# Four layers of attention and feed-forward on one Trainium2 core: layer 3's token norm, slot norm and start of the slots' loop rearranged

## The chip, the cores and the metric

The kernel runs on one NeuronCore of a Trainium2 chip. The metric is the device time of one execution in microseconds (us); lower is better. Engines are named as in the profile: PE (matrix multiply), PEld (its weight loads), DVE (VectorE), ACT (ScalarE), POOL (GpSimd), SP (SyncE, here only DMA issue).

## The reference

Four layers, each `xn = layernorm(x)` and then `x = x + attention(xn) + ffn(xn)`, on 8 batches of 512 tokens with 128 channels. The change is in the last layer and in the end of the one before:

```
xn = layernorm(x)                                  # layer 3's first norm
x  = x + L3_attn(xn) + L3_ffn(xn)

def L3_attn(x):     # channel attention, 16 heads of 8 channels
    q, k, v = split(x @ qkv_w.T + qkv_b)
    k = layernorm(k, 8 channels of a head); v = the same
    kv  = k.T @ v / 512 * temperature + attn_bias  # 8 x 8 for each head
    att = q @ kv + x
    return gelu(att @ p1_w.T + p1_b) @ p2_w.T + p2_b + x

def L3_ffn(x):      # soft mixture of 16 experts with 64 slots each
    x  = layernorm(x) * norm_g + norm_b            # a second norm of the same tokens
    se = (layernorm(slot_embeds) * slot_g + slot_b) * scale
    logits   = x @ se.T                            # 512 tokens x 1024 slots
    dispatch = softmax(logits, over tokens)
    combine  = softmax(logits, over slots)
    slots = dispatch.T @ x                         # then 16 gated experts on the slots
    return combine @ experts(slots)
```

## The kernel before

The whole state stays in SBUF: X (128 x 32 x 128), XN its norm, XT the norm transposed. Every engine has a queue of its own, written out by hand as a loop over **steps**. In a step the functions of one engine stand one behind the other, and an engine takes its instructions in order. Semaphores join the engines. Products of a softmax's stage are made as three fp32r matmuls, high with high, low with high and high with low (`m3`, L161 to L163), so each operand needs a rounded high part (written by ACT, L171) and a low part (a subtraction on DVE or POOL, L181).

**Layer 2** has `NV2 = 256` score tiles, one in a step (32 a batch). For tile v: PE scores in step v, DVE the negated row maximum (`minus_max`, L193) in v+1, ACT the exponential with its sum (L167) in v+2, DVE the reciprocal (L1631) in v+3, the normalising product in v+4 (DVE L176 or POOL L176 by turns), PE four transposes (L335) in v+5, ACT the high part (L171) in v+6, DVE the low part (L181) in v+7, PE the product with the values four steps later. Once a batch, beside these, stand layer 3's first norm of that batch (`STAT3`, `ROOT3`, `SCALE3`, `TOKENS3` steps behind `OT_AT`) and its transposes into XT.

**Layer 3's slots' loop** starts at step `S3 = NV2 + 2` and overlaps layer 2's last steps. It works on 64 tiles (8 a batch) of 128 slots by 512 tokens with the same software pipeline: `scores` at step v, `soft` v+1, `exp` v+2, `rec` v+3, `norm` v+4, `p_tr` v+5, `hi` v+6, `lo` v+7, `pv` from v+10, where step numbers are shifted by `LEAD = 33`. `scores(v)` waits until `exp(v-2)` has read its PSUM bank, since there are two banks (`S_BANK`). One of four `norm` is on POOL and three are on DVE. Into the same steps tables put each batch's **front**: the attention of layer 3 and the second norm, whose pieces are told by name and whose numbers are steps, shifted by 8 a batch:

```
F_PE = {0: "q", 1: "kv0", 2: "kv1", 14: "km", 17: "kq", 19: "p1", 21: "p2", 28: "tr"}
F_DV = {2: "kv0", 3: "kv1", 4: "s1", 8: "v1", 10: "vn", 15: "km", 18: "ta", 22: "x2", 23: "nv", 25: "xn", 30: "lo"}
F_AC = {1: "qt", 7: "sq", 9: "root", 20: "gelu", 24: "root2", 29: "hi", 30: "xnh"}
F_PO = {0: "x1", 5: "vs", 11: "gb", 26: "ngb", 31: "lo"}
```

`kv0`, `kv1` are keys and values with their bias (DVE). `s1` sums the heads of 8 channels (L189) and `vs` subtracts their mean on POOL (128 x 1024). `sq`, `v1`, `root`, `vn` scale them by the root of the variance: `root` is a Sqrt on ACT, and `newton` (L208 and the rows behind it) a reciprocal and one Newton step. `gb` applies gain and bias on POOL, `km`, `kq`, `ta`, `p1`, `gelu`, `p2`, `x2` are the attention's products and the sum into X. `nv`, `root2`, `xn`, `ngb` are the second norm of the tokens, with statistics of its own (L200, L203). `tr`, `hi`, `lo` make the operand of the scores (XTr, XL3), `xnh` and POOL's `lo` that of `pv`. `x1` adds the norm and p2's bias to X. The slots' embeddings are treated once, in `stat`, `sroot`, `snorm`, `saff`, `st`, `shi`, `slo`. The loop has `LEAD + 64 + 15 = 112` steps. Behind it come the experts' stage and the combine stage, each with a loop of its own. SP issues the layer's 14 loads (L1915) when batch 6's last scores of layer 2 are through.

## Time and profile before

| | us |
|---|---|
| median of 3 runs | 2239.09 (2236.21 to 2239.7) |
| the profiled execution | 2235.8 |
| its span, first to last instruction | 2234.0 |
| PE busy | 1940.2 (87%) |
| DVE busy | 1759.8 (79%) |
| ACT busy | 1420.7 (64%) |
| POOL busy | 1235.4 (55%) |
| mean granted TensorE clock | 0.963 |

Busy time is the time in which an engine had at least one instruction in work. A share over the whole span averages stages with different limits, so stages are read one by one: layer 2's last batch begins at about 1660 us of the span, the slots' loop's first score tile is at 1797.3, its last at 1998.3, the experts' stage starts at 2012.2 and the combine stage at about 2097.

### The profile page before, as it was taken

Reading aid. Unit: us, or ns where it says so; the run is one execution under the profiler, and the core shown is the slowest. Engines: PE = TensorE matmul, PEld = TensorE weight load, DVE = VectorE, ACT = ScalarE, POOL = GpSimd, SP = SyncE. Lnnn points to the kernel's source line nnn. Section 1 sums busy time; section 2 is a strip of 40 time slices with the busy share of each in tenths; the row PEclk is TensorE's granted clock in tenths of the full one; section 3 lists DMA queues with packets and bytes.
Section 4 is the critical chain, followed back from the end, with each engine's and each line's share of the span. In section 5 each row is a group of like instructions: output and inputs, shape, how many; then the busy total and the mean of one; then the engine's idle time right before and its main releaser. Section 6 shows DMA issues by size and latency. Waiting matters only on the chain.

```text
span 2234.0 us, 38976 instructions
## 1 busy us (share of the span) xinstructions
PE 1940.2 (87%) x13526; PEld 1475.1 (66%) x13526; DVE 1759.8 (79%) x4071; ACT 1420.7 (64%) x2801; POOL 1235.4 (55%) x1042
## 2 busy tenths in 40 slices
PE   3799899999989898588996999999999568789898
PEld 2566666666666666454683778778777346567797
DVE  8688989898888888467187888888888899873586
ACT  2578677777878777244235666667666257766575
POOL 3778777787877776157053445554445465326300
PEclk9999999999999999689997999999999789999999
DMA  3998788888888885201000000000010000002000
GB/s 105 310 312 303 260 299 284 291 280 291 279 290 284 289 300 211 86 1 37 1 6 1 1 1 1 1 1 1 1 32 1 0 0 1 1 31 69 24 1 39
DMA packets 73875, 264.14 MB, mean 118 GB/s; under 512 B 12272, under 2 KB 32240, under 8 KB 73168
## 3 DMA queue, kind: packets, MB, share of 16 engines
q1 hardware_dynamic: 72880, 255.19, 33.9%
q10 hardware_dynamic: 800, 6.46, 0.8%
q8 instruction: 109, 1.79, 0.3%
q14 instruction: 86, 0.70, 0.1%
HBM read 140.30 MB, written 121.31 MB: 117 GB/s over the span
## 4 chain that ended last, share of the span: by engine, by line
PE 39%; DVE 8%; ACT 6%; issue 2%; POOL 2%; POOLq 0%; DVEq 0%; ACTq 0%
PE PS L157 10%; PE PS L161 8%; PE PS L163 7%; PE PS L162 7%; PE PS L335 7%; ACT AR L167 2%; DVE AR L181 2%; ACT L167 1%; DVE DR L181 1%; DVE AR L185 1%; DVE PT L181 1%; ACT AR L171 1%; ACT PT L171 1%; POOL AR L176 1%; DVE AR L200 0%
## 5 line engine op out<-in xcount | busy, mean ns | idle before, releaser
L167 ACT ACTIVATE AR<-PS,AR 128x512 f32<-128x512 f32 x1008 | 687.3, 689 | 285.2 <-DVE AR L193 192.3
L193 DVE TENSOR_REDUCE AR<-PS 128x1 f32<-128x512 f32 x896 | 615.9, 688 | 119.0 <-PE PS L163 101.1
L335 PE MATMUL PS<-ident,AR 128*128 128x128 f32 x3816 | 584.4, 277 | 69.9 <-DVE PT L181 23.6
L157 PE MATMUL PS<-AR 128*9 128x512 f32 (+8 forms) x4190 | 507.7, 361 | 101.2 <-DVE AR L181 40.4
L335 PEld LDWEIGHTS PS<-ident,AR 128*128 128x128 f32 x3816 | 433.9, 142 | 182.6 <-issue 67.4
L181 POOL TENSOR_TENSOR AR<-AR 128x512 f32<-128x512 f32 (+5 forms) x326 | 396.9, 1234 | 254.8 <-DVE AR L181 96.0
L157 PEld LDWEIGHTS PS<-AR 128*9 128x9 f32 (+5 forms) x4190 | 292.3, 134 | 307.2 <-DVE AR L181 137.9
L171 ACT ACTIVATE AR<-PS 128x512 f32<-128x512 f32 (+3 forms) x612 | 357.1, 588 | 91.0 <-PE PS L335 47.6
L176 POOL TENSOR_SCALAR AR<-AR 128x512 f32<-128x512 f32 x144 | 245.3, 1704 | 290.3 <-DVE AR L1631 215.9
L171 ACT ACTIVATE PT<-PS 128x512 fp32r<-128x512 f32 x320 | 191.4, 598 | 196.2 <-PE PS L335 159.1
L181 DVE TENSOR_TENSOR PS<-PS,AR 128x192 f32<-128x192 f32 (+1 forms) x512 | 201.4, 393 | 99.3 <-PE PS L544 92.4
L181 DVE TENSOR_TENSOR AR<-PS,AR 128x512 f32<-128x512 f32 (+3 forms) x321 | 209.9, 654 | 34.8 <-PE PS L157 31.4
L181 POOL TENSOR_TENSOR AR<-XN,AR 128x192 f32<-128x192 f32 (+1 forms) x170 | 201.7, 1208 | 45.2 <-DMA XN<-scr 36.8
L181 DVE TENSOR_TENSOR PT<-PS,PT 128x512 fp32r<-128x512 f32 x320 | 217.4, 680 | 3.5 <-ACT PT L171 3.5
L544 PE MATMUL PS<-AR 128*128 128x320 bf16 (+3 forms) x1024 | 196.6, 274 | 0.0
L181 POOL TENSOR_TENSOR AR<-AR,XN 128x512 f32<-128x512 f32 x144 | 154.4, 1075 | 67.5 <-DVE AR L181 64.9
L541 PE MATMUL PS<-ident,XN 128*128 128x128 f32 x680 | 130.0, 273 | 0.0
L161 PE MATMUL PS<-MH,XNr 128*128 128x512 f32 x256 | 123.5, 482 | 5.2 <-ACT AR L167 2.8
L176 DVE TENSOR_SCALAR AR<-AR 128x512 f32<-128x512 f32 (+6 forms) x229 | 117.8, 518 | 1.3
L544 PEld LDWEIGHTS PS<-AR 128*128 128x128 bf16 x1024 | 100.8, 98 | 6.1
L161 PE MATMUL PS<-PT,VW 128*128 128x512 f32 x256 | 102.3, 399 | 1.8 <-DVE PT L181 1.8
L163 PE MATMUL PS<-MH,XNr 128*128 128x512 f32 x256 | 102.0, 398 | 0.0
(161 smaller groups left out, 2984.5 us busy)
## 6 DMA issues: line engine op xcount, KB each, us to landing
scr<-AR SPq DMA_DIRECT2D x128, 800.0 KB, 4.4
XN<-scr SPq DMA_DIRECT2D x85, 768.0 KB, 6.7
AR<-scr SPq DMA_DIRECT2D x43, 768.0 KB, 6.5
AR<-qsc SPq DMA_DIRECT2D x96, 192.0 KB
qsc<-AR SPq DMA_DIRECT2D x96, 128.0 KB, 3.3
AR<-in_wgu SPq DMA_DIRECT2D x16, 256.0 KB, 3.2
X<-in_x ACTq DMA_DIRECT2D x1, 2048.0 KB, 8.5
AR<-in_wi ACTq DMA_DIRECT2D x1, 2048.0 KB, 7.8
```

Of the source, the lines that this page charges most:

```text
L157: return pe.e.matmul(out, lhsT, rhs, start=start, stop=stop)
L161: pe.e.matmul(out, l[0], r[0], start=start, stop=False)
L162: pe.e.matmul(out, l[1], r[0], start=False, stop=False)
L163: return pe.e.matmul(out, l[0], r[1], start=False, stop=stop)
L167: return ac.e.activation(out, in_, func, bias=bias, scale=scale, accum_out=accum)
L171: return ac.e.activation(out, in_, ACT.Copy, bias=0.0, scale=1.0)
L176: return en.e.tensor_scalar(out, in0, s1, None, op0)
L181: return en.e.tensor_tensor(out, in0, in1, op)
L193: return dv.e.tensor_reduce(out, in_, AX.X, ALU.max, negate=True)
L335: return pe.e.transpose(out, in_, ident[0:k, 0:k])
L541: pe.e.matmul(out, lhsT, rhs, start=start, stop=start, is_transpose=True, skip_group_check=True)
L544: return pe.e.matmul(out, lhsT, rhs, start=False, stop=stop, skip_group_check=True)
```

## The change

- **First norm and second norm in layer 2's steps.** The second norm is no longer taken from statistics of its own. The tokens normed once have mean 0 and variance v y y (v the variance, y the root's reciprocal), so `scales` works out a second factor yy3 from them, POOL takes its root by a power, and ACT multiplies XN by it (`second`). ACT also sets X to X + norm (`sums`), which was half of `x1`. The steps of all this stand in `at3(b)`.
- **Gain and bias of the second norm** are applied on the transposed tokens (one column each), in the ACT copy `hi` and in a DVE operation `z` from PSUM; the difference `lo` goes to POOL. The slots take them in the copy out of PSUM. `nv`, `root2`, `xn`, `ngb` and one load are gone.
- **Keys and values are centred by their weights:** `wc` subtracts the head mean from the weights and the bias once, and `s1` and `vs` are gone.
- **Roots:** `root` is Ln and then Exp with scale -0.5 on ACT; `newton3` has three DVE operations where `newton` had five with a reciprocal.
- **Slots' embeddings** are treated in 30 steps ahead of S3, between layer 2's tiles (`PRE3`, and the entries with negative steps).
- **`LEAD` is 9 where it was 33**, so the loop has 88 steps. `norm` is on DVE for two tiles of four, POOL one, ACT one.
- Tiles have other places in SBUF, the banks of transposes and of `pv` are others, and a third store (XTX) holds operands of the scores.

```diff
-        STAT3, ROOT3, SCALE3, TOKENS3, TR3 = 2, 3, 5, 6, 11
+        STAT3, ROOT3, SCALE3, ROOT33, SCALE33 = 2, 3, 5, 6, 8
+        def at3(b):
+            if b < NB - 1:
+                return (6, 7, 8, 9), 11, 12, (13, 14, 15, 16), (17, 18, 19, 20)
+            return (6, 6, 6, 6), 7, 8, (9, 9, 10, 10), (11, 11, 12, 12)
-        S3 = NV2 + 2
+        S3, PRE3 = NV2 + 2, 30
...
                 dv.step(newton3(dv, y3, v3, q3))
                 dv.settle()
-                stt(dv, off3, NMV[:, 4 * b:4 * b + 4, 0], -1.0, y3, ALU.mult, ALU.mult).then_inc(n_y, 1)
+                dv.step(tt(dv, yy3, y3, y3, ALU.mult))
+                stt(dv, off3, NMV[:, 4 * b:4 * b + 4, 0], -1.0, y3, ALU.mult, ALU.mult)
+                ts(dv, up3, y3, 1.0, None, ALU.add).then_inc(n_y, 1)
+                dv.settle()
+                dv.step(tt(dv, yy3, yy3, NMV[:, 4 * b:4 * b + 4, 1], ALU.mult))
+                dv.settle()
+                ts(dv, v3, yy3, 1e-5, None, ALU.add).then_inc(n_v, 1)
+            def scales2(b):
+                newton3(dv, yy3, v3, q3).then_inc(n_y, 1)
...
+                    if r == sums[q]:
+                        act(ac, xt, xt, ACT.Identity, bias=off, scale=up3[:, q:q + 1])
+                    if r == second[q]:
+                        ins = act(ac, nt, nt, ACT.Copy, scale=yy3[:, q:q + 1])
...
-        LEAD, NV3 = 33, 8 * NB
+        LEAD, NV3 = 9, 8 * NB
...
-        F_PE = {0: "q", 1: "kv0", 2: "kv1", 14: "km", 17: "kq", 19: "p1", 21: "p2", 28: "tr"}
+        F_PE = {0: "tr", 2: "q", 3: "kv0", 4: "kv1", 13: "km", 15: "kq", 24: "p1", 26: "p2"}
+        F_DV = {2: "z", 4: "kv0", 5: "kv1", 7: "v1", 10: "vn", 14: "km", 16: "ta", 27: "x2"}
+        F_AC = {1: "hi", 3: "qt", 6: "sq", 9: "root", 10: "xnh", 25: "gelu"}
+        F_PO = {3: "lo", 5: "pb", 11: "gb", 13: "polo"}
+        I_PE = {0: "st0", 1: "st1"}
+        I_DV = {-29: "wc", -19: "sagg", -16: "snewt", 2: "slo0", 3: "slo1"}
+        I_AC = {1: "shi0", 2: "shi1"}
+        I_PO = {-26: "sgs", -18: "sroot", -10: "sm0", -8: "sa0", -6: "sm1", -4: "sa1"}
+        for i in range(8):
+            I_DV[i - 27], I_AC[i - 15] = f"ss{i}", f"sn{i}"
...
-        S_BANK, T_BANK = (5, 6), (7, 3)
+        S_BANK, T_BANK = (5, 6), (3, 4)
...
-                if 0 <= v - 4 < NV3 and (v - 4) % 4 != 1:
+                if 0 <= v - 4 < NV3 and v % 2 == 0:
                     norm(v - 4)
...
                 elif what == "root":
-                    ins = act(ac, SM[b % 2][:, 2, :], SM[b % 2][:, 1, :], ACT.Sqrt)
+                    ac.step(act(ac, tm, SM[b % 2][:, 0, :], ACT.Ln))
+                    ac.settle()
+                    ins = act(ac, tm, tm, ACT.Exp, scale=-0.5)
...
+                elif what == "z":
+                    ins = ts(dv, XL3f[:, sl], PS[:, f_bank["tr", b], :], ncol[:, 0:1], ncol[:, 1:2], ALU.mult, ALU.add)
```

How the instructions stand, at two places. PE, from layer 2's last products with the values (PT, VW) to layer 3's first score tile (operand SEH). Before:

```order
L163 MATMUL PS<-PT_01_61,VW_57 128x512
L157 MATMUL PS<-XT,AR 128x512
L335 MATMUL PS<-ident,AR 128x128 x4
L157 MATMUL PS<-AR,XT 128x256 x2
L335 MATMUL PS<-ident,AR 128x128 x4
L157 MATMUL PS<-AR,XT 128x256 x2
L157 MATMUL PS<-AR 128x128 x4
L157 MATMUL PS<-XT,AR 128x512
L157 MATMUL PS<-AR 128x512
L157 MATMUL PS<-AR,XT 128x256 x4
```

Behind the first row these are the first nine of the nineteen rows that stood between the two; now:

```order
L163 MATMUL PS<-PT_01_61,VW_57 128x512
L335 MATMUL PS<-ident,XN 128x128 x4
L161 MATMUL PS<-XTX,SEH 128x512
L162 MATMUL PS<-XTX,SEL_67 128x512
L163 MATMUL PS<-XL_71,SEH 128x512
```

One batch's four transposes are left between them. ACT in the steady loop, where a batch's `root` stands (128x128; PT is a tile's high part, `PS,AR 128x512` an exponential or, behind a table load and ahead of the root, the gelu). Before:

```order
L167 ACT_TABLE_LOAD
L167 ACTIVATE AR<-AR 128x4
L171 ACTIVATE PT_00_69<-PS 128x4x128
L167 ACT_TABLE_LOAD
L167 ACTIVATE AR<-PS,AR 128x512
L167 ACT_TABLE_LOAD
L167 ACTIVATE AR<-AR 128x128
```

Here the two roots (128x4 and 128x128) have an exponential and a high part between them, and the gelu stands some steps away with two loads of its own. Now:

```order
L171 ACTIVATE PT_00_69<-PS 128x4x128
L167 ACTIVATE AR<-PS,AR 128x512
L167 ACT_TABLE_LOAD
L167 ACTIVATE AR<-PS,AR 128x512
L167 ACT_TABLE_LOAD
L167 ACTIVATE AR<-AR 128x128
L167 ACT_TABLE_LOAD
L167 ACTIVATE AR<-AR 128x128
```

The gelu, Ln and Exp stand directly behind each other, each with a table load ahead of it, and no load stands between this Exp and the next exponential: three loads a batch where there were six.

## Rows read from the trace of the kernel before

**Rows 1.** The page, busy time, share and instructions of each engine.

```profile
PE 1940.2 (87%) x13526; PEld 1475.1 (66%) x13526; DVE 1759.8 (79%) x4071; ACT 1420.7 (64%) x2801; POOL 1235.4 (55%) x1042
```

**Rows 2.** Windows: length, busy (x count) of PE PEld DVE ACT POOL, clock, DMA.

```profile
1659.97:1724.40 64.43, 62.42 (x346) 51.10 (x345) 54.73 (x132) 44.43 (x105) 32.25 (x21) 1.00 0.07 21
1724.40:1797.30 72.90, 41.32 (x149) 28.59 (x148) 61.58 (x133) 21.04 (x33) 37.60 (x23) 0.74 0.00 0
1797.30:1998.60 201.30, 159.75 (x765) 119.27 (x764) 178.18 (x430) 144.97 (x271) 95.15 (x59) 0.94 0.03 9
1998.60:2012.20 13.60, 11.19 (x56) 8.23 (x54) 6.67 (x15) 6.50 (x14) 1.72 (x1) 1.00 0.00 0
```

**Rows 3.** Tiles VW and SEH: min/median/max ns, first and last start in us.

```profile
L163 PE MATMUL PS<-PT,VW x256: 387/392/628, 1233.6 to 1748.4; 128*128 128x512 f32 x128
L161 PEld LDWEIGHTS PS<-XTr,SEH x64: 186/190/337, 1797.3 to 1998.3; 128*128 128x128 f32 x64
```

**Rows 4.** Windows of one steady period of the slots' loop (8 steps).

```profile
1877.17:1905.37 28.20, 23.00 (x114) 16.90 (x114) 27.05 (x65) 22.08 (x40) 14.39 (x9) 1.00 0.00 1
```

**Rows 5.** Timeline of PE (start, duration in us), within one step.

```profile
1867.48 0.60 PE L335 MATMUL PS<-ident,AR 128*128 128x128 f32 x4
1867.83 0.48 PE L161 MATMUL PS<-XTr,SEH 128*128 128x512 f32 x1
...
1868.62 0.60 PE L335 MATMUL PS<-ident,XN 128*128 128x128 f32 x4
```

**Rows 6.** Timeline of ACT beside one token operation of layer 2's steps.

```profile
1703.12 0.49 ACT L167 ACTIVATE XN<-X,AR 128x128 f32<-128x128 f32 x1
...
1703.80 0.60 ACT L171 ACTIVATE PT<-PS 128x512 fp32r<-128x512 f32 x1 [0.19 <-PE PS L335]
```

**Rows 7.** Timeline of DVE and PE, layer 3's statistics between layer 2's tiles.

```profile
1695.43 0.87 DVE L200 BATCH_NORM_STATS2 AR<-X 128x6 f32<-128x128 f32 x4
...
1697.66 0.63 PE L335 MATMUL PS<-ident,AR 128*128 128x128 f32 x4 [0.90 <-DVE PT L181]
...
1699.70 0.47 DVE L176 TENSOR_SCALAR AR<-AR 128x512 f32<-128x512 f32 x1
```

**Rows 8.** Timeline of SP and DVE around the layer's loads.

```profile
1663.13 0.43 SPq L1915 DMA_DIRECT2D AR<-in_slots  x1
...
1666.87 0.69 DVE L176 TENSOR_SCALAR AR<-PS 128x512 f32<-128x512 f32 x1 [0.41 <-PE PS L157]
```

**Rows 9.** DMA issues, 1600 to 1760: size, median us from issue to landing.

```profile
AR<-in_slots SPq DMA_DIRECT2D x1, 512.0 KB, 4.5
```

**Rows 10.** Groups on DVE by form, 1848.84 to 1877.17: count | busy us, mean ns | idle.

```profile
L176 DVE TENSOR_SCALAR AR<-AR 128x512 f32<-128x512 f32 x6 | 4.4, 728 | 0.0
L189 DVE TENSOR_REDUCE AR<-AR 128x128 f32<-128x1024 f32 x2 | 2.4, 1209 | 0.0
L177 DVE TENSOR_SCALAR XN<-XN,AR 128x128 f32<-128x128 f32 x4 | 1.1, 341 | 0.0
L208 DVE RECIPROCAL AR<-AR 128x128 f32<-128x128 f32 x1 | 0.9, 936 | 0.0
L200 DVE BATCH_NORM_STATS2 AR<-XN 128x6 f32<-128x128 f32 x4 | 0.9, 276 | 0.0
L181 DVE TENSOR_TENSOR AR<-AR 128x4 f32<-128x4 f32 x3 | 0.8, 257 | 0.1
```

**Rows 11.** Groups on ACT and POOL by form, the same stretch.

```profile
L167 ACT ACT_TABLE_LOAD x6 | 7.7, 1283 | 0.1
L171 ACT ACTIVATE XNH<-XN 128x512 fp32r<-128x512 f32 x1 | 0.6, 645 | 0.0
L181 POOL TENSOR_TENSOR AR<-AR 128x1024 f32<-128x1024 f32 x3 | 6.8, 2262 | 4.4 <-DVE AR L181 2.6 <-DVE AR L176 1.8
L181 POOL TENSOR_TENSOR X<-X,XN 128x512 f32<-128x512 f32 x1 | 1.3, 1271 | 0.0
```

**Rows 12.** Waits, 1848.84 to 1905.37: us in total, times, longest us.

```profile
PE PS L161 <- ACT AR L167: 6.6, 8, 1.2
```

More of the change, by code:

```diff
@@ L1425, in program @@
         nst2 = A2.take(4, 6)
-        v3, q3, y3, off3, half3 = (A2.take(4) for _ in range(5))
+        assert A2.top <= 39440
+        A2.top = 39440
+        v3, q3, y3, off3, up3, yy3 = (A2.take(4) for _ in range(6))
+        half = A2.take(8)
+        nst, nmv, ny, nv_, ntm, soff = A2.take(8, 6), A2.take(8, 2), A2.take(8), A2.take(8), A2.take(8), A2.take(8)
+        cm = A2.take(64)
         XTb = XT[:, :].rearrange("p (b t) -> p b t", b=NB)
@@ L1756, in l2_po @@
             po.wait_ge(ld[2], 48)
-            po.step(po.e.memset(half3, -0.5))
+            po.step(po.e.memset(half, -0.5))
             po.settle()
@@ L1894, in program @@
+        in_turn = lambda at: [use for u in range(-PRE3, STEPS3) for use in at[u]]
+        cnt_pe, cnt_dv, cnt_ac, cnt_po = ({use: i + 1 for i, use in enumerate(in_turn(t))} for t in (at_pe, at_dv, at_ac, at_po))
+        taken_by = in_turn(at_pe)
         f_bank = {use: i % 3 for i, use in enumerate(taken_by)}
@@ L1927, in front @@
                     pe.wait_ge(ld[3], NL3)
-                if what == "q":
+                if what == "tr":
+                    pe.wait_ge(n_xd, V3 + 2 * b + 2)
+                    for q in range(4):
+                        ins = tr(pe, ps[:, q * 128:q * 128 + 128], XN[:, 4 * b + q, :])
+                elif what == "q":
                     pe.wait_ge(n_xt, XT3 + b + 1)
@@ L2083, in front @@
+                elif what[:2] == "ss":
+                    i = int(what[2])
+                    ins = dv.e.bn_stats(nst[:, i, :], SE[:, i, :])
+                elif what == "sagg":
+                    dv.wait_ge(f_dv, cnt_dv["ss7", 0])
+                    for i in range(8):
+                        dv.step(dv.e.bn_aggr(nmv[:, i, :], nst[:, i, :]))
                     dv.settle()
                     ins = ts(dv, nv_, nmv[:, :, 1], 1e-5, None, ALU.add)
-                elif what == "snorm":
-                    dv.wait_ge(f_ac, cnt_ac["sroot", 0])
-                    dv.wait_ge(f_dv, cnt_dv["stat", 0])
-                    dv.step(newton(dv, ny, nv_, ntm))
+                elif what == "snewt":
+                    dv.wait_ge(f_dv, cnt_dv["sagg", 0])
+                    dv.wait_ge(f_po, cnt_po["sroot", 0])
+                    dv.step(newton3(dv, ny, nv_, ntm))
@@ L2089, in front @@
                     dv.settle()
[L2090 to L2098 removed]
+                    ins = stt(dv, soff, nmv[:, :, 0], -1.0, ny, ALU.mult, ALU.mult)
@@ L2206, in step @@
                     exp(v - 2)
+                if 0 <= v - 4 < NV3 and v % 4 == 3:
+                    m = (v - 4) % 8
+                    ac.wait_ge(s3_rc, v - 3)
+                    act(ac, PB3[(v - 4) % 4], PB3[(v - 4) % 4], ACT.Copy, scale=DN3[:, m:m + 1]).then_inc(nd3_ac, 1)
                 for what, b in at_ac[u]:
```

326 lines of the change are left out of this document (173 added, 153 removed).

## Prediction

> **What bounds the kernel now.** The busy shares of the whole span [rows 1] name PE first, but they average stages with different limits. So the windows by stage come next [rows 2]. In layer 2's last batch PE is busy 62.4 of 64.4 us: PE bounds that stage, one step takes 2.01 us, and DVE has 9.7 us free there, ACT 20. In the 72.9 us behind it PE is busy 41.3 us, at a granted clock of 0.74 of 2.4 GHz, ACT 21.0 and DVE 61.6. That is a gap: layer 2's last product starts at 1748.4 and layer 3's first score tile at 1797.3 [rows 3], and between them stands little but the fronts of the first batches, a chain in which DVE is taken most. In the 201.3 us of score tiles DVE is busy 178.2. The reading is sharper in one period of 8 steps, which is one batch [rows 4]: 28.20 us, DVE busy 27.05, PE 23.0, ACT 22.1, POOL 14.4. DVE bounds the loop. PE's 23.0 holds its short waits in part, since a matmul's end is modelled: from start to start, four transposes take 0.35 us and a product of three matmuls 0.79 us [rows 5]. By that a step's own products are 0.35 + 2 x 0.79 = 1.93 us, or 15.4 a period, and the front adds about 6, which makes 21, against the 23.0 of the window; I take 22 as PE's work in a period.
>
> **The sum, stage by stage**, against the profiled execution's own 2235.8 us.
>
> *Layer 2's steps.* ACT gets eight token operations more a batch (`sums`, `second`). A token operation takes 0.49 us, and behind one of today's ACT still sat idle 0.19 us for PE [rows 6], so one in a step costs nothing, and `at3` puts them one to a step; if that cover were gone, it would be up to 0.3 us each. DVE gets 8 small operations more a batch, at about 0.2 us each with their waits. Today's statistics of a batch, 1.45 us more in one step, made PE wait 0.90 us [rows 7]; the new ones are 1.0 us in one step and 0.6 three steps on, and I take 0.3 us a batch, 2.4 in all. POOL's second power falls into the half of its steps where it has no product. The slots' work ahead of S3 adds: `wc` some 1.5 us of DVE in one step, `sagg` 1.2, `snewt` in the same step as batch 6's statistics, and four steps in which ACT has two extra operations. Each is paid in part: 2 us. `wc` and POOL's `sgs` wait for all loads, and behind `wc` stand layer 2's next row maxima, so a late load would stop PE. The last load issues at 1663.13 today and one load fewer makes it about 0.5 us earlier [rows 8]; it lands 4.5 us later [rows 9], at 1667.2. `wc` stands one step behind the operation at 1666.87 [rows 8], so at about 1669: hidden, with 1.5 us to spare. Sum: **+4 us**, between 0 (all hidden, as ACT's is) and +12 (every DVE addition paid in full).
>
> *The gap.* What stands ahead of the first score tile now is layer 2's last ten products (10 x 0.7), its last transposes, one batch's front up to `kv1`, the slots' transposes and the second batch's `tr`: 12 us of PE work from 1724.4 by the spacings of [rows 5]. The chain beside it (transposes, `hi`, `z`, POOL's `lo`) is short, since statistics, roots and slots are done. With hand-overs I take 18.6 us, so the first tile at **1743**, not 1797.3. Ends: 1736 (PE's work alone) and 1750 (right behind where the last product stands today [rows 3]).
>
> *The loop's first 15 steps* (tiles 0 to 14, fronts filling up, layer 2's last batch of statistics and tokens between them): DVE has 33 us there by the groups' durations. I take **37 us**, between 30 (layer 2's step) and 53 (today's period).
>
> *Six steady periods*, to tile 63. On DVE go from each period [rows 10]: the second norm's statistics and products (0.9 + 1.1 + 0.8, and 1.0 of small ones), one of two sums over heads (1.2 + 0.2), the reciprocal of 128 x 128 and a product behind it (1.1 net), two of six normalising products (1.46). `lo` goes and `z` comes, from PSUM and of the same size. That is 27.2 - 7.8 = 19.4 us. On ACT three table loads go (3.85), a small root goes; two copies of 128 x 512 for a product each come (1.3, by XNH's row) and Ln for 0.3: 22.1 to 19.9 [rows 4, 11]. On POOL one of three 128 x 1024 goes (2.26), `x1`'s half (1.27), and `ngb`, two of that size (2.6), and `lo`, one of it, comes [rows 11]: 14.4 a period [rows 4] becomes about 12 at most. On PE nothing goes. So PE, with 22 us, is the longest, and DVE and ACT stand at 19 to 20 close below. What is late next is the exponential. In one step of eight ACT has gelu, Ln and Exp behind one another with three loads, some 5.8 us with `hi` (3 x 1.283, two operations of the size of XNH's and two of 0.3), where today two loads at most stood between two tiles' work. `scores(v)` waits for `exp(v-2)`, and DVE's `vn` waits for the root. Followed step by step from the end of PE's `p1`, PE would reach its fourth step at 8.6 us and the exponential that it needs comes at 11.1; two steps on it has caught up to a loss of about 2 us. POOL then has `gb`, `lo`, `pb` and `polo` (8.4 us) ahead of a normalising product, which costs PE about half a microsecond more. So **24.5 us** a period, **147** for six, between 21.9 (DVE with its wait for the root) and 28.2 (nothing gained).
>
> *The tail.* From the last score tile to the experts' stage 13.6 us [rows 2]; now `p1`, gelu and `p2` of two batches stand in it: **15 us**.
>
> The experts' stage would start at 1743 + 37 + 147 + 15 = 1942, plus 4, so 1946, where it starts at 2012.2. That is 66 us less. The stages behind it keep their instructions. The profiled time becomes 2235.8 - 66 = 2169.8. The runs shown have a median 3.3 us above the profiled execution, so I predict **2173 us**.
>
> **Two rules of the Trainium skill.** The rows give 1283 ns for a table load [rows 11], and the order of instructions has one ahead of the Ln and one ahead of the Exp, three a batch. The Trainium skill, "ScalarE: Activation LUTs", section on table sets, says that Ln and Exp share one set and need one load between them. By that rule each period would have one load less; six of them make 7.7 us, and the sum would be 2165. The instructions decide, so the term stands.
>
> A normalising product on DVE takes 728 ns on the mean in the loop [rows 10] and 0.47 us where POOL is not at work beside it [rows 7]. This is what the third rival rests on. The Trainium skill, "SBUF — State Buffer", holds that DVE and GpSimd share a port pair that is locked for a whole instruction, so that the loser blocks fully; by that rule the trace agrees.
>
> **The rivals.**
> - *The loop stays at today's period.* The exponential's chain (two banks, three engines in turn) bounds it and not any engine's work. For: ACT's block is the longest single hold-up so far, and PE waits for ACT's exponentials already, 6.6 us in two periods [rows 12]. Against: those waits were behind a DVE that was 96% busy. Then 1743 + 42 + 6 x 28.2 + 15 + 4 = 1973, 39 us less: **2200 us**.
> - *PE alone sets the pace,* ACT's block is caught up in full, and the fp32 work runs at a granted clock of 1.0 throughout. For: layer 2 runs at 97% PE. Then 1743 + 32 + 6 x 22 + 14 + 3 = 1924, 88 us less: **2151 us**.
> - *The port.* Each of the four normalising products left on DVE falls beside a POOL instruction of 2.26 us and waits 1.1 us for it: DVE has 19.4 + 4.4 = 23.8 us and with its wait for the root 26.5 a period. Then 1954 + 4: 54 us less, **2185 us**.
> - *Slower.* ACT's block and POOL's eight microseconds line up, so that each batch's front comes late for the one behind it and the score tiles wait once a batch for all of it. The point at which nothing is gained: 1743 + 37 + 6P + 15 + 4 = 2012.2, so P = 35.5 us. That is 13.5 us of waiting over PE's 22. The block is 5.8 us and POOL's row 8.4, which must be paid in full, one behind the other. At P = 37 the time is 2239 + 9 = **2248 us**.
>
> **How the numbers follow.** Chances: forecast 0.55 (periods of 23.5 to 26, 2167 to 2182), today's period 0.15, PE's pace 0.15, the port 0.10, slower 0.05. The range goes from 2149 (the second rival) to 2204 (the first, with the upper end of layer 2's cost); it leaves out the slower case and what lies beyond both ends. A measurement of this kernel tells 0.2%, 4.5 us, from no change. Of the slower case 0.01 lies within that. Faster by over it is 0.95, the same 0.01, slower 0.04.
>
> **What the changed kernel's profile would show.** Right: the first score tile between 1736 and 1750; a period of about 24.5 us with PE busiest and DVE under 85%; three table loads a period; the granted clock at 1.0 between layer 2 and the loop; the experts' stage beginning near 1946; layer 2's last batch at 64 to 67 us. Wrong: a wait of DVE for a load near 1668, PE idle for ACT's exponential by more than 3 us a period, or DVE's 128 x 512 products near 1.5 us each.

## The result, and the profile after

| | before | changed |
|---|---|---|
| median (lowest to highest) | 2238.16 us (2236.21 to 2239.7, 4 runs) | 2209.34 us (2207.55 to 2211.95, 4 runs) |
| ratio, 95% interval | | 0.9873 (0.9855 to 0.989) |
| span of the profiled execution | 2234.0 | 2206.1 |
| mean granted TensorE clock | 0.963 | 0.961 |

The change gains 28.8 us, 1.3%. Forecast were 66 us: the sign was right, the size was not, and the time lies 5 us outside the range. The page's first line of the changed kernel, beside [rows 1], shows where work went: 64 us less on DVE, 18 more on ACT, 21 less on POOL.

```profile
PE 1930.2 (87%) x13526; PEld 1470.1 (67%) x13526; DVE 1695.3 (77%) x3928; ACT 1438.9 (65%) x2874; POOL 1214.8 (55%) x1033
```

The same tiles as in [rows 3], of the changed kernel (duration min/median/max in ns, first and last start in us): the last product of layer 2, the score tiles of batches 0 to 2 and of 3 to 7, and the experts' first copies.

```profile
L163 PE MATMUL PS<-PT,VW x256: 387/392/402, 1235.7 to 1745.2; 128*128 128x512 f32 x128
L161 PEld LDWEIGHTS PS<-XTX,SEH x24: 186/190/337, 1745.8 to 1822.7; 128*128 128x128 f32 x24
L161 PEld LDWEIGHTS PS<-XTr,SEH x40: 186/190/289, 1825.8 to 1963.0; 128*128 128x128 f32 x40
L171 ACT ACTIVATE HV<-AR x32: 612/620/635, 1984.0 to 2053.2; 128x512 fp32r<-128x512 f32 x32
```

From these starts the difference comes apart:

| stage | before | changed | difference |
|---|---|---|---|
| to the first score tile | 1797.3 | 1745.8 | -51.5 |
| first to last score tile | 201.0 | 217.2 | +16.2 |
| last score tile to the experts' first copy | 13.9 | 21.0 | +7.1 |
| from there to the end | 221.8 | 222.1 | +0.3 |
| sum | | | -27.9 |

So the gap ahead of the tiles closed as forecast, and 23 of its 51 us were given back behind it. The stretches of the changed kernel, in windows (length; busy us and count of PE, PEld, DVE, ACT, POOL; clock; DMA share; GB/s): the first 15 tiles, the six periods to the last tile, and the tail. DVE, busy 27 of 28 us in [rows 4], is no longer the bound of the periods: 118.33 of 170.40 us. In the first 15 tiles it is still the busiest engine, with 38.21 of 46.80.

```profile
1745.80:1792.60 46.80, 36.11 (x159) 26.20 (x158) 38.21 (x91) 34.88 (x72) 24.27 (x15) 0.85 0.00 1
1792.60:1963.00 170.40, 138.46 (x672) 107.46 (x671) 118.33 (x242) 119.01 (x225) 69.08 (x40) 0.93 0.00 1
1963.00:1984.00 21.00, 14.77 (x79) 11.16 (x77) 7.40 (x15) 12.80 (x20) 1.72 (x1) 1.00 0.17 52
```

The six periods take 28.4 us each, as long as the 28.2 of [rows 4], with another engine in front. One of them, windowed between two score tiles that follow the block of table loads:

```profile
1853.09:1880.46 27.37, 21.93 (x115) 17.08 (x114) 20.08 (x42) 20.22 (x38) 11.96 (x7) 1.00 0.00 1
```

PE's work is the 22 us that the prediction took, and DVE and ACT stand at 20 as forecast. What is left is idle time of PE: over the six periods it is idle for 31.9 us, all of it in waits for ACT's exponential. The timeline of PE has it, three waits a period for ACT's exponential, in square brackets at the row's end:

```profile
1860.18 0.50 PE L161 MATMUL PS<-XTr,SEH 128*128 128x512 f32 x1 [3.49 <-ACT AR L167]
...
1865.00 0.50 PE L161 MATMUL PS<-XTr,SEH 128*128 128x512 f32 x1 [0.98 <-ACT AR L167]
...
1876.21 0.50 PE L161 MATMUL PS<-XTr,SEH 128*128 128x512 f32 x1 [0.98 <-ACT AR L167]
```

3.49 + 0.98 + 0.98 = 5.45 us, and 21.93 + 5.45 is the window. ACT in the same step:

```profile
1853.09 1.28 ACT L167 ACT_TABLE_LOAD   x1
1854.38 0.69 ACT L167 ACTIVATE AR<-PS,AR 128x512 f32<-128x512 f32 x1
1855.09 1.28 ACT L167 ACT_TABLE_LOAD   x1
1856.38 0.31 ACT L167 ACTIVATE AR<-AR 128x128 f32<-128x128 f32 x1
1856.71 1.28 ACT L167 ACT_TABLE_LOAD   x1
1858.00 0.31 ACT L167 ACTIVATE AR<-AR 128x128 f32<-128x128 f32 x1
1858.22 0.76 ACT L167 ACTIVATE XTr<-PS,AR 128x512 fp32r<-128x512 f32 x1
1858.88 0.58 ACT L171 ACTIVATE PT<-PS 128x512 fp32r<-128x512 f32 x1
1859.36 0.69 ACT L167 ACTIVATE AR<-PS,AR 128x512 f32<-128x512 f32 x1
```

These are gelu, Ln and Exp with a load ahead of each, `hi` of the tokens, `hi` of the transposes, and then the exponential of 1859.36, on which PE's tile at 1860.18 waits: 6.3 us from the first load to it.

There is one more loss. Windows of the step behind that wait, in four periods one after the other:

```profile
1831.41:1837.64 6.23, 5.25 (x21) 4.07 (x21) 4.47 (x8) 1.78 (x5) 5.70 (x3) 0.76 0.00 0
1860.18:1865.00 4.82, 3.84 (x20) 2.82 (x20) 4.37 (x8) 1.79 (x5) 4.29 (x2) 1.00 0.00 0
1887.56:1894.02 6.46, 5.48 (x20) 3.69 (x21) 4.38 (x8) 1.79 (x5) 5.93 (x3) 0.74 0.00 1
1916.58:1922.89 6.31, 5.33 (x20) 4.15 (x21) 4.46 (x8) 1.78 (x5) 5.79 (x3) 0.75 0.00 0
```

The same work takes 4.82 us at a granted clock of 1.00, and 6.2 to 6.5 where the mean granted clock of the step is 0.74 to 0.76, that is, part of it at 1.2 instead of 2.4 GHz. Three of these four steps pay 1.4 to 1.6 us. The same step one period before them (1801.3 to 1808.9) took 7.60 us at 0.62. Work, waits and clock make the 28.4 us of a mean period: 21.9 + 5.45 + about 1. That mean holds a lighter last period of 26.3 us; the other five take 28.8, of which the clock is then about 1.5.

### The profile page after: what moved, and what is told of

Its sections match the earlier page's. It is cut to its first block, busy times and chain, and to the rows that moved or that the text cites. A ratio compares the mean times of both kernels' runs of the same rounds, so it can differ in the third digit from the quotient of the medians.

```text
span 2206.1 us, 38904 instructions
## 1 busy us (share of the span) xinstructions
PE 1930.2 (87%) x13526; PEld 1470.1 (67%) x13526; DVE 1695.3 (77%) x3928; ACT 1438.9 (65%) x2874; POOL 1214.8 (55%) x1033
## 4 chain that ended last, share of the span: by engine, by line
PE 41%; ACT 6%; DVE 5%; issue 2%; POOL 1%; DMA 0%; POOLq 0%; DVEq 0%; ACTq 0%; SPq 0%
PE PS L157 11%; PE PS L161 8%; PE PS L335 7%; PE PS L163 7%; PE PS L162 7%; ACT AR L167 3%; ACT L167 1%; ACT PT L171 1%; DVE DR L181 1%; DVE AR L185 1%; DVE PT L181 1%; POOL AR L176 1%; ACT AR L171 1%; POOL X L181 0%; DVE AR L200 0%
## 5 line engine op out<-in xcount | busy, mean ns | idle before, releaser
L167 ACT ACTIVATE AR<-PS,AR 128x512 f32<-128x512 f32 x1024 | 698.1, 689 | 288.1 <-DVE AR L193 191.6
L157 PE MATMUL PS<-AR 128*9 128x512 f32 (+8 forms) x4190 | 502.0, 360 | 86.6 <-DVE AR L181 38.0
L181 POOL TENSOR_TENSOR AR<-AR 128x512 f32<-128x512 f32 (+6 forms) x331 | 396.6, 1214 | 257.5 <-DVE AR L181 103.1
L171 ACT ACTIVATE AR<-PS 128x512 f32<-128x512 f32 (+3 forms) x596 | 347.4, 587 | 85.2 <-PE PS L335 46.9
L176 POOL TENSOR_SCALAR AR<-AR 128x512 f32<-128x512 f32 (+1 forms) x146 | 246.4, 1688 | 281.9 <-DVE AR L1643 199.4
L181 DVE TENSOR_TENSOR PS<-PS,AR 128x192 f32<-128x192 f32 (+1 forms) x512 | 201.4, 393 | 99.9 <-PE PS L544 93.0
L181 DVE TENSOR_TENSOR AR<-PS,AR 128x512 f32<-128x512 f32 (+3 forms) x321 | 210.2, 655 | 37.4 <-PE PS L157 33.7
L181 POOL TENSOR_TENSOR AR<-XN,AR 128x192 f32<-128x192 f32 (+1 forms) x170 | 201.5, 1206 | 50.5 <-DMA XN<-scr 41.2
L181 DVE TENSOR_TENSOR PT<-PS,PT 128x512 fp32r<-128x512 f32 x320 | 217.8, 681 | 13.2 <-ACT PT L171 13.0
L181 POOL TENSOR_TENSOR AR<-AR,XN 128x512 f32<-128x512 f32 x144 | 154.3, 1074 | 66.3 <-DVE AR L181 63.4
L162 PE MATMUL PS<-MH,XL 128*128 128x512 f32 x256 | 101.1, 395 | 0.0
```

Of the source, the lines that this page charges most:

```text
L157: return pe.e.matmul(out, lhsT, rhs, start=start, stop=stop)
L162: pe.e.matmul(out, l[1], r[0], start=False, stop=False)
L167: return ac.e.activation(out, in_, func, bias=bias, scale=scale, accum_out=accum)
L171: return ac.e.activation(out, in_, ACT.Copy, bias=0.0, scale=1.0)
L176: return en.e.tensor_scalar(out, in0, s1, None, op0)
L181: return en.e.tensor_tensor(out, in0, in1, op)
```

## The experiments

The theory after the result: **PE is the longest engine of the loop, so it can't make up any wait, and the time that it waits behind ACT's block of three table loads, with the slow clock around it, is lost once a batch.** Rivals: the ring of scores, maximum, exponential and transposes sets the period whatever PE does; the shorter lead of the scores (`LEAD` 9 for 33) gains nothing itself; the clock is a matter of its own. All times below come with their own runs of the kernel before; ratios are against it, and the changed kernel stands at 0.9873.

**1. No table loads.**

```diff
-                    ac.step(act(ac, tm, SM[b % 2][:, 0, :], ACT.Ln))
+                    ac.step(act(ac, tm, SM[b % 2][:, 0, :], ACT.Tanh))
-                    ins = act(ac, HG, PS[:, f_bank["p1", b], :], ACT.Gelu, bias=cols3[:, 1:2])
+                    ins = act(ac, HG, PS[:, f_bank["p1", b], :], ACT.Tanh, bias=cols3[:, 1:2])
```

> The changed kernel with Tanh in the place of Gelu and of Ln in layer 3's front: the three table loads of a period are gone, every other instruction keeps its place and size (the output is not the reference's). Theory (ACT's block of gelu, Ln and Exp with three loads holds up the exponentials, and PE cannot catch up what it idles): the wait of 3.5 us falls to under 0.5, the period from 27.4 to 23.5 to 24 us, the time by 26 to 30 us to about 2181. Rival 1 (the chain scores, maximum, exponential through two banks sets the pace whatever ACT does between): the period stays within 0.5 us of 27.4 and the time within 5 us of 2209. Rival 2 (PE catches up in the steps behind a hold-up, so its length hardly counts): a gain of under 10 us.

Measured 2172.68 us (2168.45 to 2173.56), ratio 0.9708 (0.9694 to 0.9722): 36.7 us faster than the changed kernel. More than the 26 to 30 us expected. Tanh stands where Gelu and Ln stood, so this kernel leaves out the gelu and the right roots and serves for its time alone. First to last score tile 180.6 us (217.2); the first 15 tiles, which the expectation left out, give 5.8 of it (41.0 for 46.8). A period, in a window, and the wait in the gelu's step:

```profile
1841.83:1865.30 23.47, 21.90 (x114) 17.00 (x114) 19.73 (x41) 16.08 (x35) 11.82 (x8) 1.00 0.00 1
1889.17 0.50 PE L161 MATMUL PS<-XTr,SEH 128*128 128x512 f32 x1 [0.73 <-ACT AR L167]
```

PE's busy time is the same 21.90; its wait in the gelu's step is 0.73 us, one of 0.98 is left, and the clock is at 1.00. 37 us is more than the loads' own 31 us (8 x 3 x 1.28), and about as much as the whole error of the forecast. That the period can fall to 23.5 us rules out a ring that sets 28.4 whatever ACT does between.

**2. The root by a power on POOL** instead of ACT's Ln and Exp, 128x128 in one instruction, with its wait for `v1`.

```diff
-                elif what == "root":
-                    ...
-                    ac.step(act(ac, tm, SM[b % 2][:, 0, :], ACT.Ln))
-                    ac.settle()
-                    ins = act(ac, tm, tm, ACT.Exp, scale=-0.5)
+                elif what == "root":
+                    ...
+                    ins = tt(po, SM[b % 2][:, 1, :], SM[b % 2][:, 0, :], bc(half[:, 0:1], [128, 128]), ALU.pow)
```

> The changed kernel with the root taken by a power on POOL (128x128) where Ln and Exp stood on ACT; two loads a period are left, both of the gelu. Theory: the block falls by 1.9 us (one load, Ln and Exp), PE's longest wait from 3.5 to about 1.6 us, the period to 25.5, the time by about 15 us to 2194, if the power takes under 3 us of POOL. Rival 1 (two banks): no change within 5 us. Against both: a power on 128x128 that takes POOL over 5 us a batch would hold gb and km up and make the kernel slower.

Measured 2299.62 us (2294.51 to 2300.72), ratio 1.0275 (1.0259 to 1.029): slower by far. POOL's timeline:

```profile
1860.96 20.75 POOL L181 TENSOR_TENSOR AR<-AR 128x128 f32<-128x128 f32 x1 [4.97 <-DVE AR L177]
```

One power takes 20.75 us, 0.16 us a column, and the periods become 38 to 40 us. The kernel is slower, as the expectation had it for a power of over 5 us. Its time says nothing of the theory, since POOL now holds everything up; it shows that POOL is no place for this root. PE's wait behind the gelu's two loads that are left is 1.66 to 1.68 us, near the 1.6 expected.

**3. The gelu four steps from the root.**

```diff
-        F_PE = {0: "tr", 2: "q", 3: "kv0", 4: "kv1", 13: "km", 15: "kq", 24: "p1", 26: "p2"}
+        F_PE = {0: "tr", 3: "kv0", 4: "kv1", 6: "q", 13: "km", 15: "kq", 28: "p1", 30: "p2"}
-        ... 27: "x2"}
-        F_AC = {1: "hi", 3: "qt", 6: "sq", 9: "root", 10: "xnh", 25: "gelu"}
+        ... 31: "x2"}
+        F_AC = {1: "hi", 6: "sq", 7: "qt", 9: "root", 10: "xnh", 29: "gelu"}
```

> The changed kernel with p1, gelu, p2 and x2 four steps later (and q two to four steps later, so that its buffer is free): the block becomes two, root with two loads and gelu with two loads, four loads a period. Theory (a hold-up costs PE what it exceeds some 2.3 us by): waits of 1.6 and 0.9 us where 3.5 stood, the period 1 us shorter, the tail 3 us longer, so the time 3 to 7 us shorter, about 2204. Rival (what counts is ACT's total, now one load more): 1.3 us more a period, the time 10 us longer.

Measured 2199.92 us (2198.21 to 2203.1), ratio 0.9835 (0.982 to 0.985): 9.4 us faster, more than the 3 to 7 expected, with four loads a period in place of three. PE's waits are 2.3, 0.6 and 0.98 us a period, 3.9 in all for 5.45. The waits expected of the two blocks were 1.6 and 0.9 us; the first is longer. So the number of loads is not what counts here, but how much of them stands in one block ahead of an exponential.

**4. The root by Sqrt and a longer Newton step on DVE.** Ln, settle and Exp become one Sqrt, `newton3` becomes `newton` (5 operations in place of 3).

```diff
-                    ac.step(act(ac, tm, SM[b % 2][:, 0, :], ACT.Ln))
-                    ac.settle()
-                    ins = act(ac, tm, tm, ACT.Exp, scale=-0.5)
+                    ins = act(ac, tm, SM[b % 2][:, 0, :], ACT.Sqrt)
...
-                    dv.step(newton3(dv, y1, v1, tm))
+                    dv.step(newton(dv, y1, v1, tm))
```

> The changed kernel with that one part undone: Sqrt on ACT and the reciprocal with five operations on DVE in the place of Ln, Exp and three operations. Theory: loads and block nearly the same (0.3 us less on ACT, 1.2 us more on DVE, before z): within 5 us of 2209. Rival (DVE's work still sets the pace): 1.2 us a period, 10 us longer, 2219.

Measured 2206.7 us (2204.15 to 2209.11), ratio 0.9863 (0.9847 to 0.988): 2.6 us less, which these runs don't tell from nothing. The load back to the exponential's table now stands behind both `hi`, and it is a load all the same; PE's longest wait is 3.3 us for 3.5. DVE has room for the longer step.

**5. The scores 33 steps behind the first front step again** (`LEAD, NV3 = 33, 8 * NB`), all else as changed.

> The changed kernel, with the scores 33 steps behind the slot layer's first step again, as before the change, instead of 9; everything else of the change stays. Theory (the gain of the change lies in the shorter lead, and part of it is given back because the last 24 steps now have the token work beside them): first slot tile at 1785 to 1797 us (1745.8 in the changed kernel); from first to last tile 200 to 206 us (217.2), since three periods lose their token work; the experts' first copy 14 us behind the last tile (21.0), since the token work is long over when the last tile comes; in all 15 to 27 us slower than the changed kernel, 2224 to 2236 us. Rival (the gain lies in the instructions taken out of the slot layer, not in the lead): from first to last tile 190 us or less, and within 8 us of the changed kernel, 2203 to 2217 us.

Measured 2230.51 us (2226.56 to 2233.12), ratio 0.9969 (0.9956 to 0.9982): 21 us slower than the changed kernel, so three quarters of the change's net gain are its shorter lead. The first tile comes at 1800.5 us, no earlier than before the change, although DVE has less to do there. Fronts alone are a chain of hand-overs: in 55 us PE is busy 33, at a clock of 0.66, and nobody is full.

```profile
1745.00:1800.00 55.00, 33.20 (x94) 19.96 (x93) 30.45 (x60) 26.70 (x41) 27.24 (x17) 0.66 0.00 1
```

The loop is 191.6 us there, shorter than the 200 to 206 expected and near the rival's 190; the whole time, 2230.51 us, lies in the theory's range and outside the rival's. So the instructions taken out do shorten the loop, by 9.4 us against the 201.0 of the kernel before, as long as the lead is the old one. The tail is 14.5 us as expected. What the shorter lead costs the loop is thus 26 us, what it costs the tail 6.5, and what it brings ahead of the first tile 55.

**6. One load less** (gelu as Tanh alone, as in 1; Ln and Exp stay).

> The changed kernel with Tanh in place of Gelu in the slot layer, so one of the three table loads of ScalarE's block is gone, and the two around the logarithm stay (the output differs). Theory (TensorE idles at the block's exponential, and the clock that falls behind that idle time is part of the price): the wait of TensorE for the exponential at that step falls from 3.5 us to 1.3 to 1.9 us, the granted clock stays at 1.00 behind it in all six periods, the period goes from 28.4 to 25 to 26.5 us, in all 13 to 22 us faster than the changed kernel: 2187 to 2196 us. Rival 1 (each load costs the same share of what the kernel without loads gained, 36.7 us over three loads): 12 us faster, 2197 us, with the clock still falling in some periods. Rival 2 (only the first load of the block, or the last, matters since TensorE waits for ScalarE wherever one is): within 4 us, 2205 to 2213 us.

Measured 2198.51 us (2193.15 to 2199.52), ratio 0.9822 (0.9801 to 0.9843): 10.8 us faster. As in experiment 1, Tanh leaves out the gelu. This is the first rival, an equal share for each load with the clock still falling in some periods, and not my 13 to 22 us. PE's timeline behind the block:

```profile
1829.00 0.50 PE L161 MATMUL PS<-XTr,SEH 128*128 128x512 f32 x1 [2.47 <-ACT AR L167]
...
1855.36 0.68 PE L161 MATMUL PS<-XTr,SEH 128*128 128x512 f32 x1 [2.46 <-ACT AR L167]
```

The wait fell by 1.0 us only, and the clock still fell in every second of these steps (windows 0.75, 1.00, 0.74, 1.00). From start to start of this tile the periods are 27.8, 26.4, 28.0, 26.4 and 27.3 us: 26.4 where the clock holds and 1.5 more where it doesn't. In the changed kernel the same five starts lie 30.1, 28.8, 27.4, 29.0 and 28.2 us apart. A load of 1.28 us taken away is thus 1.0 us of wait, and the mean of the five periods falls by 1.5 us (27.2 for 28.7), so that about half a microsecond of it is the clock, which falls in fewer of them.

**7. The experts' first weights earlier.** Their room is free once the last keys, values and skip sums are out, and not only behind `p2`:

```diff
-            sp.wait_ge(f_pe, cnt_pe["p2", NB - 1])
-            sp.wait_ge(f_dv, cnt_dv["km", NB - 1])
-            sp.wait_ge(f_po, cnt_po["gb", NB - 1])
+            sp.wait_ge(f_pe, max(cnt_pe["q", NB - 1], cnt_pe["kv1", NB - 1]))
+            sp.wait_ge(f_dv, cnt_dv["kv1", NB - 1])
+            sp.wait_ge(f_po, cnt_po["pb", NB - 1])
...
+                if e == 0:
+                    sp.wait_ge(f_po, cnt_po["gb", NB - 1])
+                    sp.wait_ge(f_dv, cnt_dv["km", NB - 1])
+                    sp.wait_ge(f_pe, cnt_pe["p2", NB - 1])
```

> The changed kernel, with the first expert's weights asked for as soon as the last key and value products and the last skip sum are done (their room is free then), instead of behind the last product of the token work. Theory (the 7 us that the stretch from the last slot tile to the experts' first copy has grown by are in part ScalarE's wait of 3.07 us for that transfer): the wait is gone, the experts' first copy comes 3 us earlier, in all 2 to 4 us faster, 2205 to 2207 us. Rival (the copy waits for something else next, the last slots' product or VectorE's last parts): within 1 us of the changed kernel, 2208 to 2210 us.

Measured 2204.23 us (2203.62 to 2206.22), ratio 0.9855 (0.9834 to 0.9877): 5.1 us less by the medians. The tail, from the last score tile to the experts' first copy, is 17.9 us for 21.0: 3.1 us, as much as the wait was and inside the 2 to 4 expected. The rest of the 5.1 lies ahead of the last tile, where the edit changes nothing (1961.5 for 1963.0). In ACT's timeline of the changed kernel the copy waits for the transfer; with the early request it waits no more, and the second copy 0.63 us.

```profile
1983.96 2.26 ACT L171 ACTIVATE HV<-AR 128x512 fp32r<-128x512 f32 x4 [3.07 <-DMA AR<-in_wgu]
```

```profile
1979.45 1.15 ACT L171 ACTIVATE HV<-AR 128x512 fp32r<-128x512 f32 x2
1981.22 1.15 ACT L171 ACTIVATE HV<-AR 128x512 fp32r<-128x512 f32 x2 [0.63 <-DMA AR<-in_wgu]
```

**8. Edits 3 and 7 together.**

> The kernel with the gelu four steps from the root (run before: 2199.9 us), and the first expert's weights asked for early as well. The two edits touch different stretches, so their gains should add: 2196 to 2198 us, faster than both kernels of the change. Rival (the last stretch of that kernel, 23.1 us, is set by the token work that now ends later, so the early transfer gives nothing): 2199 to 2201 us.

Measured 2198.11 us (2193.75 to 2201.37), ratio 0.9824 (0.9801 to 0.9846): 1.8 us less than with edit 3 alone (0.9835). The intervals overlap, so the times alone leave open whether the early request gains there. In the two traces the tail is 19.4 us (1956.1 to 1975.6) for 23.1 (1951.6 to 1974.7), which speaks against the rival: the transfer's wait of 5.82 us ahead of the first copy is gone, and one of 2.17 us for DVE's sums into X is left.

**9. The deciding one: another order on PE in one step of eight.** In the step that waits 3.5 us, `p2`, `q` and the values' product stood behind the waiting scores in PE's queue, and none of them needs the exponential.

```diff
+                late = u % 8 == 2
-                if 0 <= v < NV3:
+                if 0 <= v < NV3 and not late:
                     scores(v)
                 for what, b in at_pe[u]:
                     front(what, b)
                 g, j = divmod(v - 10, 4)
                 if 0 <= g < 2 * NB:
                     pv(g, j)
+                if 0 <= v < NV3 and late:
+                    scores(v)
```

> The changed kernel with TensorE's order changed in one step of eight, the one whose scores wait 3.5 us for the exponential behind ScalarE's three table loads: there the token work's products (second product of the gelu, queries) and the step's share of the values' product are issued ahead of the scores instead of behind them. Nothing is added or taken out. Theory (what TensorE loses in a period is that wait, since it has no slack to make it good, and the half clock behind it): these products are about 3.1 us of work that needs no exponential, so the wait falls from 3.5 us to 0.3 to 0.8 us, the granted clock stays at 1.00, and the period goes from 28.4 to 24.5 to 25.5 us; over some seven periods 20 to 27 us faster than the changed kernel, 2182 to 2190 us. Rival (the ring of scores, maximum, exponential and transposes sets the period, TensorE's idle time only shows where it is late): the scores of that step come later by what was put ahead of them, the wait moves on to the next steps, and the time is within 6 us of the changed kernel, 2203 to 2215 us.

Measured 2187.25 us (2186.86 to 2191.78), ratio 0.9776 (0.9752 to 0.9799): 22 us faster than the changed kernel, inside the 20 to 27 expected, from instructions that are the same in number and kind. PE's timeline, to be held against the rows around 1860.18 above:

```profile
1851.91 0.60 PE L335 MATMUL PS<-ident,AR 128*128 128x128 f32 x4
1852.35 1.06 PE L157 MATMUL PS<-AR 128*128 128x128 f32 x8
1853.24 1.02 PE L157 MATMUL PS<-XT,AR 128*128 128x512 f32 x2
1853.70 0.79 PE L161 MATMUL PS<-PT,XNH 128*128 128x512 f32 x1
...
1855.99 0.50 PE L161 MATMUL PS<-XTr,SEH 128*128 128x512 f32 x1 [1.04 <-ACT AR L167]
...
1857.82 0.63 PE L335 MATMUL PS<-ident,AR 128*128 128x128 f32 x4 [0.87 <-DVE PT L181]
```

The 3.5 us wait is 1.04, not the 0.3 to 0.8 expected, and 0.87 have come up at the next transposes, which wait for DVE's `lo` of the tiles. Windows of two periods one after the other:

```profile
1829.61:1855.99 26.38, 23.51 (x114) 18.02 (x114) 20.43 (x42) 20.12 (x39) 11.98 (x7) 0.94 0.00 1
1855.99:1880.74 24.75, 21.84 (x115) 16.87 (x115) 20.45 (x42) 20.14 (x39) 12.00 (x7) 1.00 0.00 1
```

Where the clock holds the period is 24.75 us, as expected, and PE's work is again 21.84. Where it falls it is 26.38. They alternate, and the mean from the tile at 1804.87 to that at 1931.19 is 25.3 us (28.7 over the same tiles of the changed kernel). The clock at 1.00 throughout was expected and did not come. The two periods at 1.00, 24.75 and the changed kernel's 27.37, differ by 2.6 us, so that much is the wait's alone, whatever the clock does; the other 0.8 of the 3.4 us is a clock that falls less often.

**10. The same order in all steps** (`late = True`).

> The same order (token products and the values' product ahead of the scores) in every step of the slot loop. Theory: the waits of 0.98 us at two other steps of a period are covered too, and the exponentials have a slack of one step that takes the later scores: 2175 to 2190 us. Rival (at the steps that wait for nothing now, the later scores bring the maximum and the exponential late, and put new waits where there were none): slower than with the order changed in one step alone, 2195 us or more.

Measured 2186.0 us (2183.32 to 2190.91), ratio 0.9771 (0.974 to 0.9801). The two waits of 0.98 us go, and small ones of 0.2 to 0.9 us at the transposes come. Against edit 9 nothing that the runs can tell; both the theory's 2175 to 2190 and the rival's mechanism hold in part.

**11. Edits 7 and 9 together.**

> The one step's new order and the first expert's weights asked for early, together: the first is worth 20 to 27 us by the theory, the second took 3 to 5 us off by itself, and they lie in different stretches, so 2178 to 2186 us; without a gain from the order (the ring as the bound) 2200 to 2210 us.

Measured 2186.82 us (2185.18 to 2188.89), ratio 0.9775 (0.9753 to 0.9796): just above the expected 2178 to 2186, and by the medians no faster than edit 9 alone (0.4 us). The tail is 17.9 us, against 20.6 with edit 9, so the early request does its part there; a difference of 3 us is too small for these medians.

**12. Edits 3, 7 and 10 together.**

> Three edits that gained by themselves, in one kernel: the gelu four steps from the root (four table loads a period instead of three, but at most two in one block), token and values' products ahead of the scores in every step, and the first expert's weights asked for early. Theory (only the length of the wait behind one block counts, and what TensorE has to put into it): at the root's step the 2.3 us wait of the kernel with the gelu apart falls to about 1.1 us, since only the values' product can be put there, at the gelu's step and the others to nothing or little; a period near 25 us, 26 with the order alone; in all 2174 to 2184 us, the fastest of the kernels with the right output. Rival (with the order changed, what is left of the waits sits on the transposes, which wait for VectorE's copies behind ScalarE's, and a fourth load makes ScalarE late at more places): 2184 us or more, no better than the order alone.

Measured 2188.74 us (2182.37 to 2193.38), ratio 0.9777 (0.9753 to 0.9801), outside the theory's 2174 to 2184. The rival was right: spreading the loads adds nothing to the order. A period is 25.5 us there, with four loads. The root's step still waits 1.35 us for the exponential and 0.87 for the transposes.

| run | median us | ratio (95%) | first, last score tile | experts' first copy | PE for ACT, 1820 to 1950: us in all, longest |
|---|---|---|---|---|---|
| changed kernel | 2209.34 | 0.9873 (0.9855 to 0.989) | 1745.8, 1963.0 | 1984.0 | 26.0, 3.5 |
| 1 no loads | 2172.68 | 0.9708 (0.9694 to 0.9722) | 1743.7, 1924.3 | 1945.1 | 9.7, 1.1 |
| 3 gelu apart | 2199.92 | 0.9835 (0.982 to 0.985) | 1743.0, 1951.6 | 1974.7 | 20.1, 2.3 |
| 5 lead 33 | 2230.51 | 0.9969 (0.9956 to 0.9982) | 1800.5, 1992.1 | 2006.6 | 24.4, 4.9 |
| 6 one load less | 2198.51 | 0.9822 (0.9801 to 0.9843) | 1747.0, 1954.7 | 1975.2 | 20.9, 2.5 |
| 9 scores last | 2187.25 | 0.9776 (0.9752 to 0.9799) | 1750.1, 1947.0 | 1967.6 | 10.7, 1.6 |
| 10 in all steps | 2186.0 | 0.9771 (0.974 to 0.9801) | 1746.9, 1943.0 | 1963.0 | 5.8, 1.3 |

The last column adds PE's waits for ACT between 1820 and 1950 us; experiment 1's loop ends inside that stretch. All four kernels with the new order beat the kernel before and the changed one, the latter by 20.6 to 23.3 us. Among them the runs don't choose.

The places in this table are those of one execution each, and they carry what came before: layer 2's first score product starts anywhere from 1208.9 (edit 3) to 1218.2 us (edits 3, 7 and 10), at 1211.2 in the changed kernel, though none of the edits touches anything ahead of it. So differences of a few microseconds between two rows can be older than the edit. From that product to the end of the span it is 994.9 us in the changed kernel, 987.5 with edit 3, 990.7 with edit 7, 974.4 with edit 9, 970.9 with 7 and 9, 972.8 with 10, 973.4 with 3, 7 and 10, and 956.8 without the loads. Counted so, the gains of the order and of the loads stand as they are, and the last run is no faster than edit 10 alone.

## Why the prediction was wrong in its size

*Layer 2's steps and the gap: right in the sum, by luck.* The first score tile was put at 1743 + 4 and came at 1745.8. The parts were off and cancelled. Layer 2's own steps, from the first to the last score product, went from 511.1 us (1209.9 to 1721.0) to 518.8 (1211.7 to 1730.5): +7.7, not +4. That was inside the range of 0 to 12. PE's waits for DVE grew by 3.7 us there (13.9 to 17.6), its busy time by 2.4 and one wait for ACT by 1.0; which of the added instructions is behind each was not taken apart. Against that the way from the last score product of layer 2 to the first tile was 15.3 us, where the forecast had 22 (1721 to 1743): the 6.6 us taken for hand-overs were nothing, since PE is busy 15.21 of those 15.30 us. And 1.8 us came from ahead of layer 2, where nothing was changed. 1.8 + 7.7 - 6.7 is the 2.8 us between 1743 and 1745.8. The loads for `wc` came later than forecast, the last at 1670.35, but so did `wc`, and DVE waited for no load, as forecast. Experiment 5 shows that the lead, and not the lighter front, closed the gap.

*The first 15 steps: 46.8 us for 37.* PE is busy 36.11 us there, so the forecast's 37 has room for its work and for none of its waits: 7.2 us for ACT's exponentials, 2.1 for DVE's low parts and 1.3 for a product on POOL. The first block of loads (Ln and Exp alone) makes PE wait 2.65 us, and the mean clock is 0.85.

*The six steady periods: 170.4 us for 147. This is the step that failed.* The engines' work held: DVE 20 us, ACT 20, PE 22. (POOL's 12 held too, though the terms listed for it come to 9.6.) The failing sentence is "two steps on it has caught up to a loss of about 2 us". At PE's fourth step I had the block's wait, if 1 us short (2.5 us; measured 3.49), and then let PE make up for part of it. It cannot: caught up can be only time in which an engine would have idled anyway, and PE, with 22 us against 20, was by then the engine that everybody waits for. All 5.45 us are paid, and the clock adds 1 to 1.5. From the numbers at hand it was 22 + 2.5 for the block + 2 x 0.8 for the other steps where ACT has more to do, as [rows 12] had them on the mean, so 26.1 instead of 24.5: over six periods 10 of the 23 us. The block's wait of 3.49 instead of 2.5 is 6 more, the clock some 6. The half microsecond for POOL's work did not show: in the six periods PE waits for nothing but ACT's exponential. Experiments 1 and 9 show it from two sides: without the loads the period is 23.5 us, and with the loads in place, but other work of PE in front of the wait, 24.75 at the same clock as 27.37. The sign named in the prediction for this error, PE idle for ACT's exponential by more than 3 us a period, is what the profile shows.

*The tail: 21.0 us for 15.* The token work that now ends beside the last tiles was costed on PE alone. Its DMA was not: the weights' request stands behind `p2` on SP's queue, and ACT waited 3.07 us for it. Experiment 7 takes 3.1 us off, down to 17.9. PE is busy 14.8 of those 17.9 us, so its work was costed rightly at 15; of the rest, 2.3 us are again waits for ACT.

*The rivals.* "The loop stays at today's period" forecast 28.2 us a period and 2200 us in all, and its time is the nearest: the period was 28.4, the rest of the difference the tail and the first steps. But its mechanism, the ring of the exponential with no engine's work as the bound, is only half of it. Reordering PE alone gave 3.4 us a period, which a ring that passes through the scores would not have given. The third rival, the port, did not come true: DVE's 24 normalising products in the six periods take 0.57 us on the mean, not the 0.47 + 1.1. Only the one in four that falls beside POOL's gain and bias of 128 x 1024 is held up, to 0.72 to 0.83 us (once 1.40). The prediction's reading of [rows 7] was wrong here: POOL is at work beside that 0.47, with a normalising product from 1699.88, and DVE loses nothing to it. What holds DVE up is POOL's sums and products of two tiles (L181): in the kernel before, a product begun at 1870.85 takes 1.14 us and ends 0.3 us behind such a one of POOL (1869.75, 1.97 us). "PE sets the pace" is nearest to what the kernel without loads shows: 23.5 us a period, where that rival had 22. That its 2172.7 us are also the forecast's 2173 is chance.

*The range.* Its upper end was added up wrongly. The first rival's 2200 with layer 2's cost at 12 instead of 4 is 2208, not 2204. The measured 2209.34 lies outside that too.

*The rule on Ln and Exp.* Each has its own load in the timeline of ACT above, 1.28 us apiece, so the 7.7 us by which that rule would have lowered the sum would have made it worse. The Trainium skill, "ScalarE: Activation LUTs", section on table sets, has the two functions in one set with one load; the trace disagrees.

## What to carry to other kernels

Once a change has moved the bound to an in-order engine, price every wait of that engine in full: it has no idle time left to make one good. Then look into its queue behind each wait for work that doesn't depend on what is late, since putting it in front cost nothing here and was worth 22 us, as much as the lead itself. In a trace, look at where the changed stretch begins before comparing places: 9 us of spread came from ahead of it here. And when work is moved beside a loop's end, ask which loads were issued behind its last instruction.

## What the runs showed of the hardware that I had not expected

- A power of 128x128 elements on POOL takes 20.75 us, where one of 128x8 takes 1.67 and one of 128x4 1.04 us: about 0.16 us for each column more.
- A switch of tables costs what the load takes: the operation behind it starts 1.29 us after the load's start.
- The granted clock fell behind short waits and not in every period. Behind 3.47 to 3.49 us of idle time it was 1.00 once, 0.74 to 0.76 three times and 0.62 once; behind 2.46 us, 0.75, 1.00, 0.74 and 1.00; behind 1.04 us (experiment 9) it was 1.00 three times and 0.74 or 0.75 twice. In the kernel without loads, with 0.73 us, it stayed at 1.00. Over these runs the length of the last wait alone does not tell whether it falls; what does stays open. A step with a granted clock of 0.74 to 0.76 takes 1.4 to 1.6 us more than the 4.8 at 1.00.
